# Split q and k parts stored from GpSimd's queue, expert shares in long runs, and x stored by groups, in a two-layer decoder

## What is computed

```
x = x + self_attention0(layernorm(x))            # 16 heads of width 8
x = x + cross_attention0(layernorm(x), ctx)      # 16 heads of width 8
x = x + experts0(layernorm(x))                   # 8 experts of 256, top 2 of sigmoid scores, one shared expert
x = x + self_attention1(layernorm(x))            # relative bias, folded heads
x = x + cross_attention1(layernorm(x), ctx, mask)
x = x + experts1(layernorm(x))                   # 8 experts of 128, top 2 of softmax, a gated shared expert
return x
```

```
routed = einsum('ne,ned->nd', combine, ye)       # combine: a token's share of each of the 8 experts
```

## Time and profile before

| | us |
|---|---|
| median of 3 runs | 1318.72 (1317.16 to 1329.15) |
| the profiled execution, its own time | 1317.7 |
| its span, mean granted clock of TensorE 0.925 | 1315.9 |
| PE busy in the span | 1162.6 |
| DVE busy | 964.6 |
| ACT busy | 756.9 |
| POOL busy | 648.1 |

### The profile page before, as it was taken

How to read it: one execution, slowest core, us unless ns; L and a number is a source line. 1 busy time by engine, 2 the same in 40 slices (tenths; PEclk the granted TensorE clock), 3 DMA queues, 4 the chain that set the end, 5 groups by cost and what they waited for, 6 DMA issues and landing times. The chain is left out here.

```text
span 1315.9 us, 33949 instructions
## 1 busy us (share of the span) xinstructions
PE 1162.6 (88%) x10468; PEld 816.8 (62%) x10468; DVE 964.6 (73%) x2103; ACT 756.9 (58%) x1729; POOL 648.1 (49%) x919
## 2 busy tenths in 40 slices
PE   3899988999869699999999798988999999748995
PEld 2556655666548577777777566666455555636774
DVE  5688888888855688888788767774677776437995
ACT  1467776777654355555555376664355665426773
POOL 7546676555533456657666501116545551314553
PEclk9989999999985899999999889997799999758997
DMA  5765678666500522211210100004555552035542
GB/s 145 158 129 120 128 139 177 138 137 127 110 26 11 126 65 64 65 38 28 64 64 0 30 18 1 0 1 77 107 109 105 106 104 55 1 74 180 173 158 64
DMA packets 88510, 112.57 MB, mean 86 GB/s; under 512 B 11760, under 2 KB 69392, under 8 KB 88384
## 3 DMA queue, kind: packets, MB, share of 16 engines
q1 hardware_dynamic: 83248, 105.68, 34.6%
q10 hardware_dynamic: 5136, 5.31, 1.7%
HBM read 88.09 MB, written 22.02 MB: 84 GB/s over the span
## 5 line engine op out<-in xcount | busy, mean ns | idle before, releaser
L1429 POOL TENSOR_TENSOR experts_shared_out<-experts_act_out,experts_share 128x512 f32<-128x512 f32 x136 | 188.5, 1387 | 140.3 <-ACT experts_act_out L1591 107.9
L1597 ACT CAST experts_hidden_hi<-experts_hidden 128x512 fp32r<-128x512 f32 x216 | 134.1, 621 | 122.4 <-DVE experts_hidden L1514 82.1
L708 DVE TENSOR_REDUCE heads_neg_max<-heads_ps_max 128x4 f32<-128x512 f32 x256 | 169.7, 681 | 47.1 <-PE heads_ps_max L885 45.2
L1533 DVE TENSOR_TENSOR experts_hidden_lo<-experts_hidden,experts_hidden_hi 128x512 fp32r<-128x512 f32 x184 | 199.3, 1083 | 1.3 <-ACT experts_hidden_hi L1597 1.1
L773 ACT ACTIVATE heads_E<-heads_ps_exp 128x512 f32<-128x512 f32 x256 | 150.4, 603 | 36.0 <-PE heads_ps_pv L907 30.4
L1591 ACT ACTIVATE experts_act_out<-experts_ps_gate 128x512 f32<-128x512 f32 x216 | 128.6, 596 | 71.6 <-PE experts_ps_gate L1645 68.3
L1514 DVE TENSOR_TENSOR experts_hidden<-experts_shared_out,experts_ps_up 128x512 f32<-128x512 f32 x136 | 92.1, 677 | 69.0 <-POOL experts_shared_out L1429 58.4
L885 PE MATMUL heads_ps_max<-QK 48*128 48x128 bf16 x1024 | 104.9, 229 | 22.2 <-DMA QK<-heads_qk_parts 17.9
L1643 PE MATMUL experts_ps_y<-experts_hidden_hi,experts_down_hi 128*128 128x512 f32 x216 | 94.3, 437 | 32.6 <-DVE experts_hidden_lo L1533 19.6
L708 DVE TENSOR_REDUCE cross_neg_max<-cross_ps_max 128x4 f32<-128x512 f32 x128 | 86.9, 686 | 49.3 <-PE cross_ps_max L885 48.8
L256 POOL TENSOR_TENSOR norm_var_eps<-norm_moments,norm_eps 128x2 f32<-128x2 f32 (+1 forms) x72 | 21.5, 298 | 169.3 <-DVE norm_moments L249 169.3
(11 more groups left out here) (230 smaller groups left out, 2948.8 us busy)
## 6 DMA issues: line engine op xcount, KB each, us to landing
experts_share<-experts_cT_dram SPq DMA_DIRECT2D x7, 2304.0 KB, 9.3
experts_share<-experts_cT_dram SPq DMA_DIRECT2D x7, 2048.0 KB, 9.3
heads_qk_parts<-heads_parts SPq DMA_DIRECT2D x32, 384.0 KB, 5.5
QK<-heads_qk_parts SPq DMA_DIRECT2D x64, 192.0 KB
QK<-heads_qk_parts SPq DMA_DIRECT2D x64, 128.0 KB
cross_qk_parts<-cross_parts SPq DMA_DIRECT2D x16, 384.0 KB, 4.6
QK<-cross_qk_parts SPq DMA_DIRECT2D x32, 192.0 KB
QK<-heads_qk_parts SPq DMA_DIRECT2D x64, 64.0 KB
```

Of the source, the lines that this page charges most:

```text
L708: nc.vector.tensor_reduce(neg_max[:, half, heads.start:heads.stop], ps_max[:, u % 2, :].rearrange("q (h k) -> q h k", h=HU), AX.X, ALU.max ...
L1429: nc.gpsimd.tensor_tensor(as_group(shared_out[c % 2][:]), as_group(act_out[b][:]), share[t.k % 2][:, :, row, :], ALU.mult).then_inc(weight ...
L1533: nc.vector.tensor_tensor(hidden_lo[b][:], hidden[b][:], hidden_hi[b][:].bitcast(F32), ALU.subtract).then_inc(lo_dve, 1)
L1597: nc.scalar.copy(hidden_hi[b][:], hidden[b][:]).then_inc(hi_ready, 1)
```

## The change

**The store of the parts** leaves SP's program (L581 goes) and stands in POOL's `split`, right behind the last instruction of the split. POOL waits first for `qk_placed`, the QK loads that last read the same DRAM buffer. The semaphores that this DMA counts are kept: they are cleared at the stage's end, but not given to a later stage.

The diff, cut to what the prediction speaks of:

```diff
@@ class Semaphores, class Stage
+    def keep(self, label):
+        self.semaphores.kept.append(self.semaphores.nc.alloc_semaphore(f"{self.name}_{label}"))
+        return self.semaphores.kept[-1]
@@ head_attention
-        qk_stored = [sem(f"qk_stored{p}") for p in range(2)]
+        qk_stored = [sem.keep(f"qk_stored{p}") for p in range(2)]
...
-                if t.k % 2 == 1 and t.has(-2 * SA + 1, 2 * NG_ALL - 2 * SA - 1):
-
-                    p = slot(t, SA)
-                    sp.wait_ge(split_step, t.group(SPLITS, (SA + 1) * SPLITS))
-                    apart(sp, t, turns_sp)
-                    need(sp, qk_placed[p], t.turn(96, 0, 2 * SA))
-                    apart(sp, t, turns_sp)
-                    sp.dma_start(qk_dram[p].ap().rearrange("c r f t -> f (c r) t"), parts[p % 2][:].rearrange("f c r t -> f (c r) t")).then_inc(qk_stored[p % 2], 16)
-
...
+                p = slot(t, FA)
+                need(pool, qk_placed[p], t.turn(96, 0, 2 * FA))
+                apart(pool, t, turns_pool)
+                pool.dma_start(qk_dram[p].ap().rearrange("c r f t -> f (c r) t"), made[:].rearrange("f c r t -> f (c r) t")).then_inc(qk_stored[p % 2], 16)
@@ experts
-        cT_dram = nc.dram_tensor(f"{name}_cT_dram", (B, SLOTS, S), F32).ap()
-
-        share = [sb(f"share{p}", [128, MG, rows, S]) for p in range(2)]
+        cT_dram = nc.dram_tensor(f"{name}_cT_dram", (NMG, SLOTS, MG, S), F32).ap()
+
+        share = [sb(f"share{p}", [128, rows, MG, S]) for p in range(2)]
...
-            sp.dma_start(share[p][:].rearrange("f b e t -> f b (e t)"),
-                         cT_dram[bass.ds(group, MG), 0:rows, :].rearrange("b e t -> b (e t)").partition_broadcast(128)
+            sp.dma_start(share[p][:].rearrange("f e b t -> f (e b t)").unsqueeze(1),
+                         cT_dram[bass.ds(group, 1), 0:rows, :, :].rearrange("g e b t -> g (e b t)").partition_broadcast(128)
                          ).then_inc(share_loaded[p], 16)
...
-                sp.dma_start(share[0][:, :, these, :], cT_dram[0:MG, these, :].partition_broadcast(128)).then_inc(semaphore, 16)
+                sp.dma_start(share[0][:, these].rearrange("f e b t -> f (e b t)").unsqueeze(1),
+                             cT_dram[0:1, these, :, :].rearrange("g e b t -> g (e b t)").partition_broadcast(128)).then_inc(semaphore, 16)
...
+                if is_last and t.has(1, NMG):
+
+                    sp.wait_ge(x_added, t.batch(1, 1))
+                    apart(sp, t, turns_sp)
+                    these = bass.ds(t.batch(MG, -MG), MG)
+                    sp.dma_start(out[these].rearrange("b s d -> s b d"), x_sb[:, these, :]).then_inc(x_stored, 16)
             pair_steps(sp, emit, FIRST, LOOP_FROM, LOOP_TO, LAST)
+            if is_last:
+                sp.wait_ge(x_stored, 16 * NMG)
...
-        @block.sync
-        def _(sp):
-            sp.dma_start(out.rearrange("b s d -> s b d"), x_sb[:]).then_inc(x_stored, 16)
-            sp.wait_ge(x_stored, 16)
```

More of the change, by code:

```diff
@@ L97, in __init__ @@
     def __init__(self, nc):
-        self.nc, self.made = nc, []
+        self.nc, self.made, self.kept = nc, [], []
     def stage(self, name):
-        def sem(label):
-            self.made.append(self.nc.alloc_semaphore(f"{name}_{label}"))
-            return self.made[-1]
-        return sem
+        return Stage(self, name)
     def clear(self):
         runs = []
-        for n in sorted(s.num for s in self.made):
+        for n in sorted(s.num for s in self.made + self.kept):
             if runs and n == runs[-1].stop:
@@ L1258, in pair_steps, with experts @@
         emit(Turn(None, k))
-def experts(nc, sem, name, x_sb, norm, ident, QK, w, matrices, layer):
+def experts(nc, sem, name, x_sb, norm, ident, QK, w, matrices, layer, out=None):
     sigmoid_top2, is_last = layer == 0, layer == 1
@@ L1428, in emit @@
                         need(pool, hidden_ready, t.batch(C, c + 1 - 2))
-                        nc.gpsimd.tensor_tensor(as_group(shared_out[c % 2][:]), as_group(act_out[b][:]), share[t.k % 2][:, :, row, :],
+                        nc.gpsimd.tensor_tensor(as_group(shared_out[c % 2][:]), as_group(act_out[b][:]), share[t.k % 2][:, row, :, :],
                                                 ALU.mult).then_inc(weighted, 1)
@@ L1457, in did @@
                 dve.wait_ge(route_step, step)
+            by_expert = combine[:, :, 0:EXP, :].rearrange("s g e b -> s g b e")
             def per_token(v):
@@ L1524, in make_hidden @@
                     dve.wait_ge(act_ready, t.batch(C, c + 1))
-                    nc.vector.tensor_tensor(as_group(hidden[b][:]), as_group(act_out[b][:]), share[t.k % 2][:, :, row, :],
+                    nc.vector.tensor_tensor(as_group(hidden[b][:]), as_group(act_out[b][:]), share[t.k % 2][:, row, :, :],
                                             ALU.mult).then_inc(hidden_ready, 1)
@@ L1686, in _ @@
             for q in range(4):
-                last = nc.tensor.transpose(ps_cT[:, q, :], combine[:, 8 * q:8 * q + 8, :].rearrange("s b e -> s (b e)"), ident[:])
+                last = nc.tensor.transpose(ps_cT[:, q, :], combine[:, 2 * q:2 * q + 2].rearrange("s g e b -> s (g e b)"), ident[:])
             last.then_inc(cT_made, 1)
             pair_steps(pe, emit, FIRST + 1, LOOP_FROM, LOOP_TO, LAST)
-def store(nc, sem, out, x_sb):
-    with nc.Block() as block:
-        x_stored = sem("x_stored")
-        @block.sync
-        def _(sp):
-            sp.dma_start(out.rearrange("b s d -> s b d"), x_sb[:]).then_inc(x_stored, 16)
-            sp.wait_ge(x_stored, 16)
 def decoder(nc, a, out):
@@ L1732, in splits, with mixture @@
                     for i, (kind, n) in enumerate(counts(layer).items())]
-        def mixture(sem, layer, made):
+        def mixture(sem, layer, made, out=None):
             name = f"experts{layer}"
-            experts(nc, sem, name, x_sb, norm, ident, QK, {c: a[f"{name}_{c}"] for c in ("router", "router_bias", "rank")}, made, layer)
+            experts(nc, sem, name, x_sb, norm, ident, QK, {c: a[f"{name}_{c}"] for c in ("router", "router_bias", "rank")}, made, layer, out)
         sems = Semaphores(nc)
@@ L1764, in decoder @@
                 sems.clear()
-                mixture(sems.stage("experts1"), 1, made)
-        store(nc, sems.stage("store"), out, x_sb)
+                mixture(sems.stage("experts1"), 1, made, out)
         sems.clear()
```

23 lines of the change are left out of this document (15 added, 8 removed).

## The result

The changed kernel takes 1279.17 us (median of 4 runs, 1276.16 to 1281.15) against 1317.94 for the kernel before beside it (4 runs, 1314.88 to 1329.15): a ratio of 0.969, 95% interval 0.963 to 0.975. That is 38.8 us less, where I forecast 26.2 less. The profiled execution took 1277.92 us.

A forecast was written before the change was run, and what follows sets the result against it. PE was busy 88% of the span, so gains must come where it stands still or runs at its lower clock. -7.5 (`heads0`) - 12.2 (shares) - 6.5 (end) = -26.2 us: 1291.5 profiled, median 1292.5, range 1281 to 1318.

The forecast's parts named there:

- The mechanism of `heads0`: In `heads0` PE waits for QK loads behind a store late in SP's queue; its data lay ready for 10.0 us.
- The size of `heads0`: Half of the 18.3 us by which 27 turns exceed 10.0 us each: -9.0 us, bounds 0 and 17.9.
- The floor of 10.0 us a turn: `heads0` from 100 to 150 us runs as it should, 10.0 us a group; 27 turns averaged 10.68.
- What is late next: In `heads0` DVE, busy 43.85 of 50 us in the regular stretch, is late next; so half the excess was taken.
- POOL's price: The store's issue holds POOL 1.3 us, bounds 0.38 and 5.5 us; hidden in the regular stretch of `heads0`.
- The cover: POOL's wait for ACT in `heads0`, 1.94 us a group, hides the issue; about 0.6 us should remain.
- the filling: Start of `heads0`, where POOL works throughout without cover: the store's issue costs +1.5 us, bounds 0 and 5.2.
- Rival 1: POOL becomes the bound of `heads0`: at an issue of 4 us, 1342 us in all; chance 0.24.
- The third rival: DVE's casts and tensor_scalars hold up POOL's issue, making it 2.4 us: `heads0` -2.9, 1297 us; chance 0.10.
- The shares: Starts of both mixtures: 4 KB runs land the head in 3.7 us, head and rest in 9.0; -12.2 us together.
- The end: Last store of x is 256 KB, landing in 2.2 us against 8.7: -6.5 us, bounds -5 and -7.
- `cross1` at nothing: `cross1` costed at nothing: its groups are longer than those of `heads0` and PE there waits for no store.

The follow-up runs named there:

- `store_act_early`: The kernel before with the parts' store issued early, on ACT's queue, in the pieces of before: 1301.11 us, ratio 0.992.
- `store_pool_late`: The kernel before with the parts' store on POOL's queue, held until the q of the next group is made: 1322.13 us, ratio 1.008.
- `shift_one_part`: The changed kernel without DVE's subtraction for the low part of the shift in `heads0`, only the rounded part sent: 1268.60 us, ratio 0.968 to the kernel before.
- `dve_one_more`: The changed kernel with one more unused memset of 128x256 on DVE a step in the head stages: 1288.94 us, ratio 0.982 to the kernel before.
- `pool_two_more`: The changed kernel with two more unused subtractions on POOL behind each parts' store: 1303.34 us, ratio 0.995 to the kernel before.
- `before_head_four`: The kernel before with four rows in the head of the shares, so runs of 2 KB instead of 1 KB: 1311.04 us.
- `x_at_end`: The changed kernel with x stored once at its end instead of group by group: 1284.47 us, ratio 0.981 to the kernel before.

## Why the prediction was right and wrong

**The mechanism of `heads0`: right.** The store in SP's queue was what PE waited for, and it is its early start that helps. `store_act_early` and `store_pool_late` show it from both sides.

**The size of `heads0`: wrong, and this is the step that failed.** "So of the 18.3 us excess I take one half, 9.0 us." What came was 20.2 us over the 27 turns (19.1 to the end of the stage), more than all of the 18.3 and more than my upper bound of 17.9, "PE's whole wait". Two things were wrong. First, there was no ground for halving. The 18.3 us were a difference of times and so held whatever the late store did to a turn, the slower clock included. The turns that were longer than the good ones were those with a wait and a spell at the lower level, and with the early store all of them fell back to the length of the others. Second, the upper bound counts only the time in which PE stood still. The kernel before also ran its matmuls at a mean clock of 0.96, and in one stretch at 0.66, which I had quoted and given no term. Of the 20.0 us between the windows above, 9.6 are busy time and 10.4 idle time. That my 9.0 lies near the idle part is chance, as it was not reckoned so. The floor of 10.0 us a turn was about right: the changed kernel needs 9.93 on the mean.

**What is late next: right in part.** I named DVE. `shift_one_part` shows that its chain counts, and `dve_one_more` that it bounds the stage where POOL has the weights, but not in every turn. And I used it as a reason to halve the term, which does not follow. DVE was busy 236.7 us from 60 to 340 before and 249.6 after: it had room for the gain.

**POOL's price: right.** I took 1.3 us; it is 0.91 of issue and 0.3 of waiting. The cover held: 0.46 us a group were left from 100 to 150 us, 0.67 from 100 to 300 (13.4 us in 20 groups), where I had forecast about 0.6. I took +1.5 for the filling, and it came out at -0.7 (the 64.47 of the earlier trace rows is 63.77 now). Rival 1 did not come, and by `pool_two_more` 1.72 us more of work on POOL would have eaten the gain of `heads0`. But POOL does not bound every turn there, as the rival had it; the loss came in four stretches, with TensorE's clock down beside each.

**The third rival, DVE in POOL's way: not seen.** None of the 32 issues took longer than 1,064 ns. By the rule of the Trainium skill ("SBUF — State Buffer", "Who interferes with whom") DVE's copies, casts and tensor_scalars can block GpSimd when they run in a 2-port mode; this trace shows none of it on the issue. It shows the reverse, below.

**The shares: right.** Forecast 3.7 and 9.0 us for head and whole, landed after 4.2 and 4.6, and 8.5. The gain was 5.7 + 6.5 by my sum. In `experts0` it is 5.5 by this pair of traces and 4.2 on the mean of all, and 6.9 in `experts1`. `before_head_four` makes "the runs of 1 KB are what differs" a shown cause.

**The end: right.** -6.5 forecast, -6.7 by `x_at_end`, the last store 2.3 us (2.2).

**`cross1` at nothing: not contradicted.** `shared1` and `cross1` together gave 1.7 us in this pair of traces, which is within what they vary by.

Put together: the terms but for `heads0` missed by under 3 us in sum, and `heads0` by 11.6. The time came out 1.8 us below my range, since its lower end let all of PE's wait go and none of the clock.

## What to carry to other kernels

A DMA's place in its queue can matter more than its shape: look for a store whose data lay ready, with its queue busy on something that belongs to another turn, and issue it from the engine that made the data, if that engine has cover for the issue. When a removed wait lies in a stretch where TensorE's granted clock is below 1.00, add the clock's share of the busy time to the gain, not the wait alone; the same holds for what an added wait costs. And a wait that is gone makes room for the next: test the suspected next bound by adding a known amount to it, but then see in which turns the loss arises, and how far the profiled execution lies from the median. A total that matches what was added can still come from one stretch.

## What the runs showed of the hardware that I had not expected

**A DMA from GpSimd's queue is packed differently.** The 48 stores, each of 768 runs of 512 B, left as 5,376 packets (the row of q0 above). In `store_act_early` ACT's queue (q10) has 42,768 packets where it had 5,136, so 37,632 for the same stores, seven times as many. The landing was the same, 4.5 and 4.4 us, and so was the gain in `heads0`.

**POOL holds up DVE, its DMA issue too.** DVE's cast and subtraction of 128x16 take 0.17 us alone, but 295 and 284 ns on the mean in `heads0`. Two pieces of the changed kernel's timelines, DVE then POOL:

```profile
163.38 0.18 DVE L740 CAST heads_shift<-heads_neg_max 128x16 bf16<-128x16 f32 x1
163.59 0.73 DVE L742 TENSOR_TENSOR heads_shift<-heads_neg_max,heads_shift 128x16 bf16<-128x16 f32 x1
```

```profile
163.44 0.91 POOL L637 DMA_DIRECT2D heads_qk_parts<-heads_parts  x1 [0.29 <-POOL heads_parts L633]
```

The subtraction, begun during the store's issue, ends at 164.32, and the issue at 164.35. From 60 to 340 us 32 of these DVE instructions took over 0.3 us, and each of the 32 ended within 0.05 us of the end of a POOL instruction that was under way when it began; in five it was the issue. Not everything is held: two casts that began 0.08 and 0.11 us behind the start of an issue (at 65.78 and 75.83 us) took 0.17 us as ever, and the subtractions behind them were held to the issue's end. In `dve_one_more` four subtractions, 13.6 us apart, took 2.01 us each. This one began 0.02 us ahead of the first of two POOL instructions and ended 0.04 us behind the second:

```profile
166.27 2.01 DVE L745 TENSOR_TENSOR heads_shift<-heads_neg_max,heads_shift 128x16 bf16<-128x16 f32 x1
```

```profile
166.29 0.74 POOL L652 TENSOR_TENSOR x_sb<-x_sb,heads_bo 128x256 f32<-128x256 f32 x1
166.97 1.27 POOL L218 TENSOR_TENSOR experts_gate_lo<-experts_whole,experts_gate_hi 128x512 fp32r<-128x512 f32 x1
```

In the kernel before the sum of these two DVE groups in this stage was larger (38.9 us against 34.8), so the store's issue did not make it worse here; about 14 of the 34.8 us are more than 120 times 0.174 us, and I take them for such waiting. How much of them the stage would give back is not shown, as no run here tried to place POOL's work around DVE's.
